# Another plan for the finishes of batches in a Mamba and expert-routing kernel: by when their rows are next written

## The chip, the cores and the metric

The kernel runs on one core of a Trainium2 chip. The time is the device time of one execution in microseconds; the median of several runs is compared. The engines are TensorE (PE; its weight loads are PEld), VectorE (DVE), ScalarE (ACT), GpSimd (POOL) and SyncE (SP, which only issues DMAs here; SPq is its queue). Each works through its own instructions in a fixed order and waits on semaphores for the others.

## What is computed

A layer over 32 batches of 512 tokens of width 256, in fp32. First a Mamba block with an MLP behind it, then eight experts with two chosen for each token, and a shared expert:

```python
x = _layernorm(x + mamba_and_mlp(x))         # conv, selective scan over 512 tokens x 16 states, gate, MLP
scores = softmax(xf @ gate_w.T); _, idx = top_k(scores, 2)
y      = silu(x @ wg[e]) * (x @ wu[e]) @ wd[e]     # for the two experts e of each token
routed = sum over the two of weight * y
shared = silu(xf @ sg.T) * (xf @ su.T) @ sd.T
x = _layernorm(x + routed + shared)
```

The scan is `h = exp(dt * A) * h + (dt * x) * B` over the tokens, for 512 channels and 16 states, then `y = sum over the states of h * C`.

## The kernel before

The 32 batches go through one after another. **The scan** of a batch has 16 states (n) times 4 blocks of 128 channels (j), 64 scan instructions on DVE (L1248, `hs`). For each, ACT makes dA (L779, `ps<-dt,A`) and POOL makes dBx for two at a time (L613, `dBx<-dtx,Bbc`, 32 a batch, three buffers). SP loads the rows of B, spread over the partitions, into four buffers Bbc (L463). TensorE turns `hs` (L991), and DVE adds it into `acc` with C (L1264). Ahead of its scans, each batch needs `dt` and `dtx` in two halves, on POOL (L597, L601), behind ACT's softplus. The steps before and behind the scan of other batches (`pre`, `post`) are interleaved with it.

**The experts.** Batches are put together in groups of 6, 6, 6, 6, 4, 2, 1, 1 (`groups`, `first` is a group's first batch). `post` scatters each token's row to two rows of `X_slots`, sorted by expert (L648, indirect DMAs on POOL). When a group is complete, DVE computes where each expert's tiles begin (the bookkeeping, `meta`), and its tiles of 128 rows go through the experts in pairs (`pairs_in`). SP loads weights `wx` and rows `xin` (L508, L514) and writes the results to `Y_slots` (L531). Groups take turns in two such arrays, so the results of a group overwrite the rows of an earlier one (`before`). Ahead of that SP waits until the rows of the earlier group's last batch have been gathered (L528).

**The finish** of a batch f is what this case is about. SP waits until the store of finish f - 1 has landed (L547), and loads what the shared expert left into the one buffer `fx` (L548). POOL adds the two results of each token to it with eight accumulating gathers from `Y_slots` (L672). ACT takes sums (L914) and squares (L708), POOL computes the scale (L577 to L586, four small operations), ACT applies it (L921) and stores to `out`. That is one SP load, twelve POOL instructions, twelve ACT operations and a store.

**The order** on each engine is fixed when the kernel is built. Every strand of work (scan, pre, post, experts, results, finish, ...) has a table of places in ticks, `AT`, and there are 64 ticks to a batch. `weave` emits the steps of all strands of an engine by 64 * b + place, where b is the period that the step is planned for; a strand never goes back, a later step stands at the place of the one before it or later. The planner fills `pairs_in[b]` and `fins_in[b]`. A period has three places for finishes (0, 1, 2), a single one takes place 0, two take 0 and 1. On POOL they are

```python
"POOL_finish": [142.4813, 143.8018, 145.8918, 147.9589, ...     # place 0: eight gathers, two small steps
                ... 182.6585, 184.3464, 186.0575, 188.6853, 189.1587, 195.0384, 195.6057, 197.2903, 204.1521, 205.4386]
"SP_finish": [140.1056, 161.3954, 177.9993]                     # the load of fx, places 0, 1, 2
```

The line that the change touches says how many finishes a period gets (L187): one, from period 23 on two, from period 27 on three, as far as batches are ready.

Of the kernel before, what the change touches and what calls it, by code (L numbers as in the profile page):

```python
# [9 lines left out]
def group_sizes(n):  # L10

    sizes = []
    for size in (1, 1, 2, 4):
        if n > size:
            sizes.append(size)
            n -= size
    while n:
        sizes.append(min(6, n))
        n -= sizes[-1]
    return sizes[::-1]  # L20
# [112 lines left out]
def build(nc, a, out):  # L133
# [5 lines left out]
    NB, T, D = a["x"].shape  # L139
# [19 lines left out]
    groups = group_sizes(NB)  # L159
    NG = len(groups)  # L160
    first = [sum(groups[:g]) for g in range(NG)]
# [11 lines left out]
    before = [g - 4 if g >= NG - 2 else g - 2 for g in range(NG)]  # L173
# [4 lines left out]
    PERIODS, PAIRS_MAX, FINS_MAX, NR = NB + 3, 12, 3, 3  # L178
    pairs_in, fins_in = [[None] * PAIRS_MAX for _ in range(PERIODS)], [[None] * FINS_MAX for _ in range(PERIODS)]
    ended, finished = 0, 0  # L180
    for b in range(first[0] + groups[0] - 1, PERIODS):
        g = min(sum(first[g] + groups[g] - 1 <= b for g in range(NG)), NG - 1)
        waiting = pairs_to[g - 1] - ended
        left = max(groups[g] - (b - first[g] + 1), 1)
        take = min(waiting, PAIRS_MAX, -(-waiting // left))
        ready = sum(groups[g] for g in range(NG - 1) if pairs_to[g] <= ended) + (groups[NG - 1] if b >= NB else 0)
        done = min(ready - finished, 1 if b < NB - 9 else 2 if b < NB - 5 else 3)  # L187

        for i in range(take):
            pairs_in[b][i * PAIRS_MAX // take] = ended + i  # L190
        for i in range(done):
            fins_in[b][i * FINS_MAX // done] = finished + i
        ended, finished = ended + take, finished + done
# [1336 lines left out]
```

## Time and profile before

| | before |
|---|---|
| median of 3 runs | 4866.85 us (4865.31 to 4877.16) |
| profiled execution | 4879.34 us, span 4877.6 us |
| DVE busy | 4230.3 us (87%) |
| TensorE busy | 4114.6 us (84%) |
| ACT busy | 3579.0 us (73%) |
| POOL busy | 3566.2 us (73%) |

The span is what the profiled execution's instructions cover; its own time is 1.7 us longer. In the rows of stretches (`A:B length`, us from the span's start) stand, for each engine, the busy time and in brackets the number of instructions, then TensorE's granted clock as a share of 2.4 GHz, the mean busy share of the DMA engines, and GB/s. In rows of the timeline stand the start, the time that the row covers, engine, line, operation, what is written and read, and how many instructions the row stands for; in square brackets the idle time of the engine ahead of it and what ended it. In rows of waits stand who waited for whom, the sum in us, how many times, and the longest.

### The profile page before, as it was taken

The numbers are of one execution on the slowest core, as the hardware profiler recorded it, in microseconds if no ns is written. First come the engines' busy times: TensorE is split into PE (matmuls) and PEld (weight loads), VectorE is DVE, ScalarE is ACT, GpSimd is POOL, SyncE is SP. The second block draws the span as 40 slices with busy tenths as digits, with TensorE's granted clock in tenths as the row PEclk, the third lists the DMA queues.
The fourth block names the chain that finished last, engine by engine and source line by source line (L and its number), as shares of the span: only waits on it lengthen the run. The fifth ranks groups of instructions, "written<-read, shape, count | busy, mean of one in ns | idle before, by whom it ended". The sixth has DMA issues, their size and how long they took to land. (4 is left out here: it accounts for less than half of the span.)

```text
span 4877.6 us, 76499 instructions
## 1 busy us (share of the span) xinstructions
PE 4114.6 (84%) x21374; PEld 2848.8 (58%) x21374; DVE 4230.3 (87%) x6070; ACT 3579.0 (73%) x6521; POOL 3566.2 (73%) x2235
## 2 busy tenths in 40 slices
PE   3788888888888888888888888888888889888878
PEld 2455555555656665656665555665556666666565
DVE  4899999888988988998899999888999888898782
ACT  4767777777767777777788777787777787677754
POOL 4667677666666677777788777878778887688865
PEclk7999999999999999999999999999999999999999
DMA  2122422434334234333333333333334553455665
GB/s 92 48 88 86 116 87 78 115 118 139 117 117 132 94 119 119 91 101 118 94 98 106 99 107 105 102 100 111 100 106 127 137 138 116 121 156 157 181 164 117
DMA packets 348901, 550.96 MB, mean 113 GB/s; under 512 B 39345, under 2 KB 197170, under 8 KB 348354
## 3 DMA queue, kind: packets, MB, share of 16 engines
q1 hardware_dynamic: 279650, 448.40, 30.3%
q0 software_dynamic: 47616, 65.17, 6.6%
q10 hardware_dynamic: 21216, 32.51, 1.8%
q8 instruction: 177, 2.90, 0.2%
q14 instruction: 242, 1.98, 0.1%
HBM read 432.26 MB, written 180.80 MB: 126 GB/s over the span
## 5 line engine op out<-in xcount | busy, mean ns | idle before, releaser
L613 POOL TENSOR_TENSOR dBx<-dtx,Bbc 128x1024 f32<-128x1024 f32 x1024 | 2462.0, 2449 | 548.6 <-DVE hs L1248 528.7
L1248 DVE TENSOR_TENSOR_SCAN hs<-ps,dBx 128x512 f32<-128x512 f32 x2048 | 2400.8, 1206 | 233.8 <-ACT ps L779 134.0
L779 ACT ACTIVATE ps<-dt,A 128x512 f32<-128x512 f32 x2048 | 1392.8, 689 | 431.5 <-DVE hs L1248 398.2
L991 PE MATMUL ps<-ident,hs 128*128 128x128 f32 x8192 | 1270.8, 286 | 473.8 <-DVE acc L1264 345.6
L991 PEld LDWEIGHTS ps<-ident,hs 128*128 128x128 f32 x8192 | 954.2, 145 | 955.9 <-DVE acc L1264 589.8
L1264 DVE SCALAR_TENSOR_TENSOR acc<-ps,C_tok,acc 128x512 f32<-128x512 f32 x1664 | 1180.2, 735 | 160.4 <-PE ps L991 148.3
L648 POOL DMA_INDIRECT X_slots<-xs,slots x248 | 247.8, 999 | 268.0 <-DVE slots L1389 203.6
L672 POOL DMA_INDIRECT fx<-Y_slots,slots x224 | 354.0, 1580 | 70.2 <-issue 41.7
L1237 DVE SCALAR_TENSOR_TENSOR xc<-ps,conv_w,xc 128x511 f32<-128x511 f32 (+2 forms) x384 | 285.9, 745 | 48.6 <-ACT xc L743 39.7
L1155 PE MATMUL ps<-xsT,wx 128*128 128x128 f32 x2432 | 316.2, 279 | 5.2 <-ACT xsT L873 4.8
L1155 PEld LDWEIGHTS ps<-xsT,wx 128*128 128x128 f32 x2432 | 295.2, 194 | 34.0 <-issue 32.2
L956 PE MATMUL ps<-xnT,w_in 128*128 128x512 f32 x512 | 262.6, 632 | 45.1 <-DVE xc L1237 44.2
L1008 PE MATMUL ps<-xnT,w_in 128*128 128x512 f32 x512 | 279.7, 649 | 0.0
L1075 PE MATMUL ps<-w_m,post_tmp 128*128 128x256 f32 x1024 | 262.2, 379 | 0.0
L1058 PE MATMUL ps<-mT,w_m 128*128 128x512 f32 x512 | 242.0, 611 | 20.1 <-ACT mT L827 20.1
L597 POOL TENSOR_TENSOR dt<-dt,dtx 128x1024 f32<-128x1024 f32 x64 | 153.4, 2397 | 138.8 <-ACT dtx L770 138.8
L1042 PE MATMUL ps<-w_out,xc 128*128 128x256 f32 x1024 | 253.3, 379 | 0.0
L743 ACT ACTIVATE xc<-ps,conv_b,conv_w 128x512 f32<-128x512 f32 x128 | 99.5, 777 | 192.3 <-PE ps L956 192.3
L1042 PEld LDWEIGHTS ps<-w_out,xc 128*128 128x128 f32 x1024 | 190.3, 190 | 23.6
L1170 PE MATMUL ps<-wx,ge 128*128 128x256 f32 x608 | 166.5, 397 | 43.9 <-DVE ge L1404 42.6
L1075 PEld LDWEIGHTS ps<-w_m,post_tmp 128*128 128x128 f32 x1024 | 184.5, 190 | 20.5
L1028 PE MATMUL ps<-ident,acc 128*128 128x128 f32 x1024 | 179.7, 278 | 0.0
(222 smaller groups left out, 6237.8 us busy)
## 6 DMA issues: line engine op xcount, KB each, us to landing
Bbc<-B_scratch SPq DMA_DIRECT2D x512, 256.0 KB, 3.9
wx<-in_experts SPq DMA_DIRECT2D x304, 384.0 KB, 4.0
Y_slots<-zeros SPq DMA_DIRECT2D x228, 256.0 KB, 4.7
xin<-X_slots SPq DMA_DIRECT2D x304, 128.5 KB, 3.3
Y_slots<-xin SPq DMA_DIRECT2D x304, 128.0 KB, 1.7
xt<-in_x SPq DMA_DIRECT2D x32, 512.0 KB, 4.5
shared<-xt ACTq DMA_DIRECT2D x30, 512.0 KB, 3.9
fx<-shared SPq DMA_DIRECT2D x28, 512.0 KB, 5.3
```

The costliest lines, as they stand in the source:

```text
L613: pool.tensor_tensor(dBx[u % 3][:], dtx[b % 2][:, 2 * h:2 * h + 2, :], Bbc[g % NBB][:, n % CH:n % CH + 1, :].broadcast_to([P, 2, T]), ALU. ...
L672: pool.indirect_dma_start(out=to_finish(f)[:, t, :], out_offset=None, in_=Y_slots[g % 2], in_offset=bass.IndirectOffsetOnAxis(ap=slots[:, ...
L779: act.activation(psA[s % 2][:], dt[b % 2][:, j, :], ACT.Exp, scale=A[:, j, n:n + 1]).then_inc(s_dA, 1)
L956: i = pe.matmul(bank(b, j)[:], w_in[:, k, j * P:(j + 1) * P], xn[:, k, :], start=(k == 0), stop=(k == KD - 1))
L991: i = pe.transpose(psH[w % 2][:, j * P:(j + 1) * P], hs[(n * CT + j) % NHB][:, t * P:(t + 1) * P], ident[:])
L1008: i = pe.matmul(psG[j % 2][:], w_in[:, k, DI + j * P:DI + (j + 1) * P], xn[:, k, :], start=(k == 0), stop=(k == KD - 1))
L1042: i = pe.matmul(psG[q][:, t * D:(t + 1) * D], c[:, k, (2 * q + t) * P:(2 * q + t + 1) * P], w_out[:, k, :], start=False, stop=(k == CT - 1))
L1075: i = pe.matmul(psG[q][:, t * D:(t + 1) * D], post_tmp[:, k, (2 * q + t) * P:(2 * q + t + 1) * P], w_m2[:, k, :], start=False, stop=(k == ...
L1155: i = pe.matmul(psE[:, o * HALF + m * P:o * HALF + (m + 1) * P], w[:, m, (2 * k + o) * P:(2 * k + o + 1) * P], xsT[:, (m * KD + k) * P:(m ...
L1237: dve.scalar_tensor_tensor(out=c[:, j, s:], in0=bank(b, j)[:, 0:T - s], scalar=conv_w[:, j, NK - 1 - s:NK - s], in1=c[:, j, s:], op0=ALU.m ...
L1248: dve.tensor_tensor_scan(hs[s % NHB][:], psA[s % 2][:], dBx[s // 2 % 3][:, s % 2, :], 0.0, ALU.mult, ALU.add).then_inc(s_scan, 1)
L1264: dve.scalar_tensor_tensor(out=o, in0=psH[w % 2][:], scalar=C_tok[b % 2][:, t, n:n + 1], in1=o, op0=ALU.mult, op1=ALU.add).then_inc(s_weig ...
```

## The change

The number of finishes in a period no longer follows from the period's number. For each group h whose results will overwrite rows of an earlier group, and that isn't complete yet, `due` holds how many finishes are still missing until that earlier group is through, and how many periods are left. The period takes the largest quotient, at least one, at most three. The tables of places, the pairs and all else stay.

```diff
         ready = sum(groups[g] for g in range(NG - 1) if pairs_to[g] <= ended) + (groups[NG - 1] if b >= NB else 0)
-        done = min(ready - finished, 1 if b < NB - 9 else 2 if b < NB - 5 else 3)
+        due = [(first[before[h]] + groups[before[h]] - finished, first[h] + groups[h] - 1 - b) for h in range(NG - 1)
+               if before[h] >= 0 and first[h] + groups[h] - 1 > b]
+        due.append((NB - finished, NB - b))
+        done = min(ready - finished, max([1] + [-(-n // max(left, 1)) for n, left in due]), FINS_MAX)
```

Batches finished in each period:

| period | 11 to 13 | 14 to 16 | 17 to 19 | 20 to 22 | 23 | 24 | 25 | 26 | 27 and on |
|---|---|---|---|---|---|---|---|---|---|
| before | 1 each | 1 each | 1 each | 1 each | 2 | 2 | 2 | 0 | 3, 3, 3, 3, 1, 1 |
| after | 2 each | 0 | 2 each | 0 | 3 | 3 | 0 | 0 | 3, 3, 3, 3, 1, 1 |

The lines behind the change move by 3 in the file, so that L597 becomes L600, L613 L616, and L672 L675. Two places on POOL, in its own order. The first is the change from batch 25 to batch 26: dt and dtx are those of batch 26, `dBx` ahead of them belongs to batch 25, and `fx<-Y_slots,slots` are gathers of a finish. Before:

```order
L648 DMA X_slots<-xs,slots 29184x257 x4
L613 TENSOR_TENSOR dBx<-dtx,Bbc 128x1024 x7
L597 TENSOR_TENSOR dt<-dt,dtx 128x1024
L601 TENSOR_TENSOR dtx<-dt,xc 128x1024
L613 TENSOR_TENSOR dBx<-dtx,Bbc 128x1024
L597 TENSOR_TENSOR dt<-dt,dtx 128x1024
```

After:

```order
L616 TENSOR_TENSOR dBx<-dtx,Bbc 128x1024 x3
L675 DMA fx<-Y_slots,slots 128x256
L616 TENSOR_TENSOR dBx<-dtx,Bbc 128x1024 x2
L675 DMA fx<-Y_slots,slots 128x256 x3
L616 TENSOR_TENSOR dBx<-dtx,Bbc 128x1024
L675 DMA fx<-Y_slots,slots 128x256
L616 TENSOR_TENSOR dBx<-dtx,Bbc 128x1024
L600 TENSOR_TENSOR dt<-dt,dtx 128x1024
L604 TENSOR_TENSOR dtx<-dt,xc 128x1024
L675 DMA fx<-Y_slots,slots 128x256 x2
L616 TENSOR_TENSOR dBx<-dtx,Bbc 128x1024
L675 DMA fx<-Y_slots,slots 128x256
```

The eight gathers of the third finish of a period (place 2) now stand there; seven of them come ahead of the first dBx of batch 26. The second place is the middle of batch 13, after the scale of the first finish. Before:

```order
L613 TENSOR_TENSOR dBx<-dtx,Bbc 128x1024 x6
L625 TENSOR_SCALAR ve_post<-mv 128x4
L626 TENSOR_SCALAR nb_post<-mv 128x4
L628 TENSOR_TENSOR rs_post<-ve_post,m_half 128x4
L630 TENSOR_TENSOR nb_post<-nb_post,rs_post 128x4
L613 TENSOR_TENSOR dBx<-dtx,Bbc 128x1024 x4
```

After:

```order
L616 TENSOR_TENSOR dBx<-dtx,Bbc 128x1024 x4
L675 DMA fx<-Y_slots,slots 128x256 x2
L616 TENSOR_TENSOR dBx<-dtx,Bbc 128x1024
L675 DMA fx<-Y_slots,slots 128x256
L616 TENSOR_TENSOR dBx<-dtx,Bbc 128x1024
L628 TENSOR_SCALAR ve_post<-mv 128x4
L629 TENSOR_SCALAR nb_post<-mv 128x4
L631 TENSOR_TENSOR rs_post<-ve_post,m_half 128x4
L633 TENSOR_TENSOR nb_post<-nb_post,rs_post 128x4
L616 TENSOR_TENSOR dBx<-dtx,Bbc 128x1024
L675 DMA fx<-Y_slots,slots 128x256
```

A second finish (place 1) has come in there, away from the change of batch; its last four gathers stand a little further on.

## Rows read from the trace of the kernel before

**Rows 1.** The page: busy time, share of the span and instructions of each engine.

```profile
PE 4114.6 (84%) x21374; PEld 2848.8 (58%) x21374; DVE 4230.3 (87%) x6070; ACT 3579.0 (73%) x6521; POOL 3566.2 (73%) x2235
```

**Rows 2.** Busy time by stretch: batches 7-12, 13-18, 25-27, 28, 29, 30.

```profile
1026.80:1901.70 874.90, 758.48 (x3974) 523.79 (x3972) 782.57 (x1108) 635.20 (x1103) 585.38 (x343) 0.97 0.38 118
1901.70:2769.60 867.90, 750.63 (x3973) 518.70 (x3972) 782.09 (x1108) 667.38 (x1223) 671.68 (x415) 0.98 0.35 103
...
3637.40:4084.80 447.40, 396.77 (x2154) 284.25 (x2154) 399.19 (x560) 361.67 (x700) 379.06 (x244) 0.97 0.48 133
4084.80:4238.50 153.70, 135.33 (x718) 96.22 (x718) 136.51 (x205) 109.40 (x194) 97.84 (x58) 0.94 0.38 112
4238.50:4398.80 160.30, 141.42 (x794) 103.24 (x794) 137.90 (x194) 126.58 (x250) 133.54 (x87) 0.98 0.59 159
4398.80:4568.60 169.80, 144.72 (x786) 105.72 (x786) 142.42 (x210) 129.56 (x258) 143.21 (x95) 0.94 0.57 154
```

**Rows 3.** Waits of DVE, batches 7 to 12, then batches 13 to 18.

```profile
DVE hs L1248 <- ACT ps L779: 33.7, 28, 2.6
...
DVE hs L1248 <- ACT ps L779: 29.1, 26, 2.7
...
DVE hs L1248 <- POOL dBx L613: 2.5, 4, 0.7
```

**Rows 4.** Busy time by stretch: batch 11, batch 12 (with bookkeeping).

```profile
1611.20:1754.20 143.00, 124.38 (x648) 85.99 (x646) 128.87 (x181) 104.44 (x182) 97.45 (x57) 0.96 0.38 117
1754.20:1901.70 147.50, 125.65 (x648) 85.46 (x646) 134.15 (x200) 104.57 (x182) 98.03 (x58) 0.97 0.34 104
```

**Rows 5.** Waits of SP's queue, 3600 to 4240 us.

```profile
SPq L547 <- DMA out<-fx: 35.3, 3, 12.0
```

**Rows 6.** Timeline of POOL around the change from batch 26 to 27.

```profile
3901.47 7.02 POOL L613 TENSOR_TENSOR dBx<-dtx,Bbc 128x1024 f32<-128x1024 f32 x3
...
3923.76 2.37 POOL L597 TENSOR_TENSOR dt<-dt,dtx 128x1024 f32<-128x1024 f32 x1 [3.31 <-ACT dtx L770]
...
3928.70 2.35 POOL L613 TENSOR_TENSOR dBx<-dtx,Bbc 128x1024 f32<-128x1024 f32 x1
```

**Rows 7.** Timeline of DVE, first scans of batch 27.

```profile
3935.16 2.33 DVE L1248 TENSOR_TENSOR_SCAN hs<-ps,dBx 128x512 f32<-128x512 f32 x2
3939.15 2.34 DVE L1248 TENSOR_TENSOR_SCAN hs<-ps,dBx 128x512 f32<-128x512 f32 x2 [1.66 <-ACT ps L779]
```

**Rows 8.** Timeline of POOL around the change from batch 29 to 30.

```profile
4362.53 6.99 POOL L613 TENSOR_TENSOR dBx<-dtx,Bbc 128x1024 f32<-128x1024 f32 x3
4369.68 1.64 POOL L672 DMA_INDIRECT fx<-Y_slots,slots  x1 [0.16 <-issue]
...
4395.77 2.94 POOL L613 TENSOR_TENSOR dBx<-dtx,Bbc 128x1024 f32<-128x1024 f32 x1
```

**Rows 9.** Timeline of DVE, first scans of batch 30.

```profile
4398.79 2.34 DVE L1248 TENSOR_TENSOR_SCAN hs<-ps,dBx 128x512 f32<-128x512 f32 x2 [2.65 <-POOL dBx L613]
4407.86 2.34 DVE L1248 TENSOR_TENSOR_SCAN hs<-ps,dBx 128x512 f32<-128x512 f32 x2 [6.73 <-issue]
```

**Rows 10.** Busy time, sixteen scans around the start of batches 27, 29, 30, 31.

```profile
3915.54:3950.71 35.17, 30.44 (x199) 23.15 (x198) 29.08 (x36) 32.80 (x52) 28.14 (x14) 1.00 0.40 122
...
4218.89:4257.17 38.28, 32.20 (x212) 24.71 (x211) 29.98 (x37) 34.58 (x58) 27.35 (x13) 1.00 0.54 158
4376.43:4421.99 45.56, 36.56 (x215) 28.02 (x214) 30.21 (x38) 39.04 (x74) 40.41 (x24) 0.89 0.60 156
4545.16:4590.57 45.41, 36.07 (x215) 27.30 (x214) 30.20 (x38) 37.12 (x66) 39.80 (x23) 0.92 0.67 182
```

**Rows 11.** Waits of SP's queue in the stretch of batch 30.

```profile
SPq L547 <- DMA out<-fx: 32.8, 3, 24.9
...
SPq L528 <- DMA fx<-Y_slots,slots: 0.7, 1, 0.7
```

**Rows 12.** Waits of SP's queue over the whole span.

```profile
SPq L528 <- DMA fx<-Y_slots,slots: 3.6, 2, 2.8
```

## The prediction, made before the result was known

> **What bounds the kernel now.** I read the page first: the share of busy time puts VectorE (DVE) at 87% over the span, TensorE at 84%, GpSimd (POOL) and ScalarE (ACT) at 73% [rows 1]. Then the span by stretches, each from the first scan of one batch to that of a later one. Six stretches with no finish (batches 7 to 12) take 874.9 us with 782.6 us of DVE work; the next six, with one finish in each batch, take 867.9 us with 782.1 us of it [rows 2]. So the length of a batch follows DVE: 130 us of work in 145. One finish puts (671.68 - 585.38) / 6 = 14.4 us on POOL and (667.38 - 635.20) / 6 = 5.4 us on ACT, none on DVE, and the batch is no longer for it. What DVE waits for says the same: in six batches with one finish it waits 2.5 us in all for POOL's dBx, and 29.1 us for ACT's dA, against 33.7 us for dA in the six without a finish [rows 3]. A finish is covered work, as long as POOL delivers dBx in time.
>
> **What moves.** The planner puts finishes planned for period b where batch b + 2 is scanned: POOL has 343 instructions in batches 7 to 12 and 415 in the next six, twelve more for each, and the first finish is planned in period 11 [rows 2]. Working through the loop, with groups of 6, 6, 6, 6, 4, 2, 1, 1 batches, gives in scanned batches: before, one finish in each of 13 to 24, two in each of 25, 26, 27, none in 28; after, two in 13 to 15, none in 16 to 18, two in 19 to 21, none in 22 to 24, three in 25 and 26, none in 27 and 28. From batch 29 on both plans are alike (18 finishes are placed by then). TensorE and DVE keep their instruction order throughout; POOL, ACT and SP change theirs. The amount of work is the same.
>
> **Edit 1: six batches get a second finish (place 1).** Place 1 exists in batches 25 to 27 now, so its price can be read there. Those three take 447.4 us, 149.1 each, with 7 pairs of expert tiles; batch 28, with 7 pairs and no finish, takes 153.7 us, of which the bookkeeping at the end of a group is 147.5 - 143.0 = 4.5 (batch 12 against 11) [rows 2, 4]. So 149.1 with two finishes against 153.7 - 4.5 = 149.2 with none: price 0. POOL has room: 379.1 of 447.4 us busy in the three [rows 2]. SP waits 35.3 us in three pieces there for the store before a reload of fx [rows 5]; what is queued behind it on SP are the loads of Bbc, wx and xin, and since the three batches are no longer than batch 28 without its bookkeeping, the four Bbc buffers cover it. Six of these at 5 pairs: I take 0, bounds -1 to +1.5 us each.
>
> **Edit 2: seven batches lose theirs.** 16 to 18, 22 to 24 and 27. The nearest rows are the stretch without finishes, 7.0 us per six longer than with them [rows 2]. That stretch also clears Y_slots (DMA share 0.38 against 0.35), so I don't read it as a gain of finishes; it only says that taking one away gives nothing visible. I take 0. The bound below is all of DVE's waiting for dA and dBx in such a batch, (29.1 + 2.5) / 6 = 5.3 us each; the bound above is 7.0 / 6 = 1.2 us each.
>
> **Edit 3: batches 25 and 26 get a third (place 2).** This is the term that isn't zero. POOL_finish starts place 2 at 182.66 ticks and ends it at 205.44, with 64 ticks to a batch, so its eight gathers stand in POOL's queue across the change from one batch to the next, where POOL must also do dt and dtx of the new batch (four operations of 2.4 us) before DVE can scan it. Now this happens twice, into batches 30 and 31. First the change into batch 27, with no place 2: from the last triple of dBx (3901.47) POOL still waits, 3.31 us just before dt, since ACT is later than it; its first dBx for the new batch ends at 3931.06, some 4.1 us before DVE takes it at 3935.16 [rows 6, 7]. Into batch 30 the same chain (from 4362.53) holds seven gathers, the first at 4369.68 (1.64 us), and dBx beside them takes 2.94 instead of 2.35 us; the first dBx for the new batch ends at 4398.71, 36.2 us after the start of the triple instead of 29.6, DVE takes it at once (2.65 us of wait), and the second half comes late: DVE is idle 6.73 us before the scan at 4407.86 [rows 8, 9]. From the first pair of scans to the second it is 9.07 us instead of 3.99 [rows 7, 9].
>
> Those stretches differ in pairs (10 against 7), so I take the price from whole stretches, eight scans either side of the change of batch [rows 10]. Into 27 (7 pairs, no place 2) it lasts 35.2 us; into 29 (10 pairs to come, no place 2) 38.3; into 30 and 31 (place 2) 45.6 and 45.4, with DVE's work the same as into 29 (30.2 against 30.0). **7.2 us for a place 2 with pairs held equal**, 10.3 with them not (45.5 - 35.2). Two of them: 14.4 us, bounds 0 and 20.6. After the change of batch a part can be won back where DVE would have waited for something else. Idle time of DVE outside that stretch: batch 29 has 160.3 - 137.9 - 8.3 = 14.1, batch 30 has 169.8 - 142.4 - 15.4 = 12.0 [rows 2, 10]. So up to 2 us a time come back: 14.4 - 4 = 10.4. On the other side stands what place 2 does to batch 26 beyond that: the reload of fx at its head must wait until ACT has stored the finish before it. In batch 30 SP waits 24.9 us for that and 32.8 in three pieces [rows 11], with Bbc, wx and xin behind it. DVE loses little there (that is inside batch 30's own 12.0), and with 7 pairs there is less behind it; I add 0 to 2 us, once, and take 1. The middle of 10.4 and 14.4 is 12.4, and with that 1 it is 13.4: **+13 us** for this edit.
>
> In the stretches into 30 and 31 TensorE's granted clock is 0.89 and 0.92, into the others 1.00, so in part of them it ran at 1.2 GHz and not 2.4, and its busy time is 36.6 us for 215 matmuls against 32.2 for 212 [rows 10]. This lies inside the 7.2 us. The Trainium skill, page "TensorE: Matmul & The Clock Gate", section "Part 1: The HAM clock gate", says that the clock falls to half after the array has been idle; by that rule the fall follows from the stall, and comes back with it at the two new places. By a clock that fell there for another reason (the 10 pairs), up to 36.6 - 32.2 = 4.4 us of each 7.2 would not recur, and the sum would be 13 - 8.8 = +4.
>
> **Edit 4: the wait that the plan is about.** Before a group's results overwrite Y_slots, SP waits for the gathers of an earlier group (L528). Such waits are 3.6 us in two pieces over the whole span; one of them, 0.7 us, is in the stretch of batch 30, where the plan doesn't change [rows 11, 12]. For groups 2, 3 and 4 the places say that the last finish is on time: SP_results starts at 99.19 ticks of period 17, which is tick 1187, and the gathers of batch 5, planned in period 16, end by tick 1174. Gain: 0.
>
> **Sum.** 0 + 0 + 13 + 0 = +13 us on the profiled execution, whose span is 4877.6 and whose own time is 4879.34. It lies 12.5 us above the median of the runs, 4866.85. On the median: 4880.
>
> **Rivals.** *Place 2 costs nothing at 7 pairs.* The stalls into 30 and 31 would belong to the pairs, the clock or the last groups. For it: batches 25 and 26 have less for SP and TensorE, and part of the extra time is TensorE's at the lower clock. Against it: the stretch into 29, and POOL's chain, which has the same order and no pair in it. Time: -3 to +6, or 4864 to 4873; it decides whether POOL reaches dt in time. *Starved by SP.* With 7 pairs DVE uses up Bbc faster than in batch 30 (149 us a batch against 165), and 25 us of SP's wait outlast the buffers; a third finish also delays the second one, and batch 26 stretches as 30 and 31 did as a whole, with 27.4 us of DVE idle instead of 15: two times 12. Time: +21 to +35, 4888 to 4902. POOL waited only briefly for Bbc in batch 30, so it is unlikely. *Faster.* Seven batches without a finish lose more than half of DVE's waiting for dA and dBx, since ACT is 5.4 us and POOL 14.4 us freer there: 7 x 3 = 21 us, less a small place 2, -10 to -25 and 4842 to 4857. It decides itself from 2 us a batch up. Against it: the 33.7 us of waits for dA in the six batches without finishes. *The plan doesn't move what it says.* The order of POOL shows that it does; no chance.
>
> **How the numbers follow.** The forecast (+6 to +20) has 0.62, nothing 0.20, starved 0.10, faster 0.08. A measurement of this kernel can tell about 0.3% from no change, 14.6 us, so the forecast lies just under that line: of its 0.62 I put 0.27 above it. Slower: 0.27 + 0.10 = 0.37; faster 0.07, a hundredth of that case falling inside; same 0.56. The range holds the forecast and nothing: 4861 to 4889.
>
> **What would show it.** Right: no waits of POOL before dt into batches 26 and 27, DVE idle some 6 us before the third scan there, both stretches of sixteen scans at 42 to 46 us instead of 35.2, TensorE's clock under 1.00 in them, batches 16 to 18 within 2 us of now, and all from batch 28 on unchanged. Wrong: those stretches at 35 to 37 us (nothing), POOL waiting for Bbc by several us in batch 26 (starved), or batches 16 to 18 and 22 to 24 at 142 us or less (faster).

## The result: slower by 0.77%, and where the time is

The changed kernel takes 4918.6 us (median of 5 runs, 4906.69 to 4924.05), the kernel before, beside it, 4873.3 us: 1.0077 times as long, 95% interval 1.0061 to 1.0094. The forecast was 4880, with a range up to 4889. The span of the profiled execution went from 4877.6 to 4917.7 us. The first line of the page of the changed kernel, which answers to [rows 1]:

```profile
PE 4134.5 (84%) x21374; PEld 2873.8 (58%) x21374; DVE 4246.6 (86%) x6070; ACT 3582.7 (73%) x6521; POOL 3567.9 (73%) x2235
```

DVE is busy for 16.3 us more with the same 6070 instructions in the same order. Nothing in the prediction accounts for that. The stretches of the changed kernel show where it is: batches 13 to 15 (two finishes each), 16 to 18 (none), 19 to 21 (two), 22 to 24 (none), and 25 to 27 (three, three, none):

```profile
1905.40:2353.90 448.50, 380.82 (x2012) 266.45 (x2010) 400.51 (x547) 353.17 (x676) 379.21 (x243) 0.97 0.42 115
2353.90:2784.90 431.00, 371.29 (x1964) 257.10 (x1962) 392.31 (x561) 315.65 (x548) 293.75 (x171) 0.98 0.28 87
2784.90:3231.50 446.60, 381.61 (x2012) 266.06 (x2010) 399.56 (x548) 353.29 (x676) 378.96 (x244) 0.97 0.42 116
3231.50:3661.10 429.60, 372.23 (x1987) 258.98 (x1986) 392.80 (x563) 316.56 (x550) 294.94 (x172) 0.99 0.29 88
3661.10:4123.30 462.20, 404.09 (x2154) 291.35 (x2154) 395.99 (x560) 361.84 (x700) 378.98 (x244) 0.96 0.46 129
```

The same stretches of the kernel before. Those of batches 25 to 27 are in [rows 2]:

```profile
1901.70:2338.30 436.60, 379.63 (x2011) 262.57 (x2010) 389.81 (x548) 335.53 (x616) 335.76 (x208) 0.98 0.36 104
2338.30:2769.60 431.30, 371.01 (x1963) 256.13 (x1962) 392.29 (x562) 331.84 (x608) 335.93 (x208) 0.98 0.35 102
2769.60:3202.30 432.70, 377.09 (x2011) 262.77 (x2010) 389.28 (x547) 335.61 (x616) 335.72 (x207) 0.98 0.36 105
3202.30:3637.40 435.10, 376.07 (x1988) 259.25 (x1986) 393.98 (x563) 332.23 (x610) 337.72 (x208) 0.98 0.36 101
```

The two runs of three batches with a second finish lose 11.9 and 13.9 us, and DVE's busy time there grows by 10.7 and 10.3. Batches 16 to 18 stay as they were (431.0 against 431.3), 22 to 24 are 5.5 us shorter. Batches 25 to 27 lose 14.8 us. The kernel before isn't at its best in these rows: TensorE's clock fell for 6.8 us in its batches 14, 15 and 21, at 2.6 to 2.9 us each (the experiments come back to this), so the second finishes cost more than 11.9 and 13.9 us. The rest, 3.7 us ahead of batch 13 and 1.6 from batch 28 on, lies where the two kernels have the same order on every engine; it is within what two executions of one kernel differ by (the spans of e4_before_psum and e9_psum_again below, one kernel, are 9.2 us apart).

Within a batch the loss of place 1 is at one point. Counting from the first scan of batch 14, the two kernels are within 0.4 us of each other up to the 41st scan; from there to the 45th it takes 27.58 us instead of the 21.7 us of batches 16, 17, 22 and 23, which have none, and of the kernel before with one finish. (The last batch of a group, 18 or 24, has the bookkeeping there and takes 26.7 to 26.8 us in both.) In the six batches with a second finish these four scans take 26.3 to 27.6 us, 30.6 us more than six times 21.65. The timeline of DVE there, changed kernel:

```profile
2147.87 0.20 DVE L1350 TENSOR_REDUCE ps<-ps 128x4 f32<-128x32 f32 x1
2148.11 0.19 DVE L1352 TENSOR_TENSOR r<-rank,ps 128x32 f32<-128x32 f32 x1
2148.33 3.10 DVE L1366 TENSOR_TENSOR chosen<-r,r 128x32 bf16<-128x32 f32 x1
2151.45 0.75 DVE L1369 TENSOR_TENSOR prefix<-prefix,chosen 128x8 bf16<-128x8 bf16 x4
...
2160.21 0.42 DVE L1289 SCALAR_TENSOR_TENSOR post_tmp<-post_tmp,ps 128x256 f32<-128x256 f32 x1 [1.32 <-ACT post_tmp L854]
```

The same step in batch 14 of the kernel before:

```profile
2139.96 0.19 DVE L1363 TENSOR_TENSOR chosen<-r,r 128x32 bf16<-128x32 f32 x1
```

And POOL over those microseconds, first the changed kernel, then the kernel before:

```profile
2146.10 5.26 POOL L616 TENSOR_TENSOR dBx<-dtx,Bbc 128x1024 f32<-128x1024 f32 x2
...
2154.53 1.08 POOL L651 DMA_INDIRECT X_slots<-xs,slots  x1 [2.94 <-DVE slots L1392]
...
2159.08 0.19 POOL L585 TENSOR_SCALAR ve_fin<-squares_fin 128x4 f32<-128x4 f32 x1 [2.19 <-ACT squared L711]
```

```profile
2133.63 2.36 POOL L613 TENSOR_TENSOR dBx<-dtx,Bbc 128x1024 f32<-128x1024 f32 x1 [0.52 <-DVE hs L1248]
2143.27 1.12 POOL L648 DMA_INDIRECT X_slots<-xs,slots  x1 [7.29 <-DVE slots L1389]
```

`chosen` adds two small tiles, `one1` and `one2`, both in SBUF. It takes 3.10 us instead of 0.19, and ends 0.06 us after POOL's second dBx (2151.36). Before, POOL had done its dBx 4 us earlier and stood idle for 7.29 us, waiting for `slots`, while DVE did this step. The eight gathers of place 1 take up POOL's idle time (2.94 us of that wait are left): POOL's last two dBx slip until they lie over `chosen`. In all six batches with a second finish (13 to 15, 19 to 21) `chosen` takes 2.98 to 3.84 us, and each time it ends 0.06 us after the second of two dBx of POOL. The wait is inside the instruction, so it is booked as busy and stands in no list of waits. The group of that line, changed kernel:

```profile
L1366 DVE TENSOR_TENSOR chosen<-r,r 128x32 bf16<-128x32 f32 x31 | 34.9, 1125 | 1.1
```

**Place 2** came as forecast. Sixteen scans around the start of batches 26, 27 and 28 of the changed kernel, which answer to [rows 10]:

```profile
3789.41:3832.89 43.48, 34.10 (x200) 25.22 (x198) 29.22 (x36) 37.48 (x70) 41.27 (x25) 0.92 0.46 119
3949.11:3992.14 43.03, 33.83 (x200) 24.91 (x198) 29.46 (x36) 37.14 (x70) 40.37 (x24) 0.92 0.57 154
4103.65:4138.81 35.16, 30.43 (x199) 23.14 (x198) 29.07 (x35) 32.77 (x52) 28.14 (x14) 1.00 0.35 106
```

43.5 and 43.0 us against 35.2, with the same work on DVE, and TensorE's clock at 0.92. Inside the first of them POOL doesn't wait before `dt`, and DVE stands idle ahead of the third scan of batch 26, as the prediction said (some 6 us):

```profile
3813.05 2.34 DVE L1251 TENSOR_TENSOR_SCAN hs<-ps,dBx 128x512 f32<-128x512 f32 x2 [2.72 <-POOL dBx L616]
3822.14 2.34 DVE L1251 TENSOR_TENSOR_SCAN hs<-ps,dBx 128x512 f32<-128x512 f32 x2 [6.75 <-issue]
```

### The profile page after: what moved, and what is told of

Read it like the earlier page. It is cut to its first block and busy times, and to the rows that moved or that the text cites. A ratio compares the mean times of both kernels' runs of the same rounds, so it can differ in the third digit from the quotient of the medians.

```text
span 4917.7 us, 76499 instructions
## 1 busy us (share of the span) xinstructions
PE 4134.5 (84%) x21374; PEld 2873.8 (58%) x21374; DVE 4246.6 (86%) x6070; ACT 3582.7 (73%) x6521; POOL 3567.9 (73%) x2235
## 5 line engine op out<-in xcount | busy, mean ns | idle before, releaser
L616 POOL TENSOR_TENSOR dBx<-dtx,Bbc 128x1024 f32<-128x1024 f32 x1024 | 2464.6, 2444 | 580.9 <-DVE hs L1251 565.1
L675 POOL DMA_INDIRECT fx<-Y_slots,slots x224 | 354.2, 1581 | 75.9 <-issue 40.5
L600 POOL TENSOR_TENSOR dt<-dt,dtx 128x1024 f32<-128x1024 f32 x64 | 155.7, 2433 | 132.1 <-ACT dtx L773 132.1
L1045 PEld LDWEIGHTS ps<-w_out,xc 128*128 128x128 f32 x1024 | 190.3, 190 | 23.6
```

What stands on the lines that cost most here:

```text
L616: pool.tensor_tensor(dBx[u % 3][:], dtx[b % 2][:, 2 * h:2 * h + 2, :], Bbc[g % NBB][:, n % CH:n % CH + 1, :].broadcast_to([P, 2, T]), ALU. ...
L675: pool.indirect_dma_start(out=to_finish(f)[:, t, :], out_offset=None, in_=Y_slots[g % 2], in_offset=bass.IndirectOffsetOnAxis(ap=slots[:, ...
L1045: i = pe.matmul(psG[q][:, t * D:(t + 1) * D], c[:, k, (2 * q + t) * P:(2 * q + t + 1) * P], w_out[:, k, :], start=False, stop=(k == CT - 1))
```

## The experiments

**The two parts of the change, one at a time.** e1_doubles keeps the new plan up to period 22, e2_triples from 23 on:

```diff
 # e1_doubles
         done = min(ready - finished, max([1] + [-(-n // max(left, 1)) for n, left in due]), FINS_MAX)
+        if b > 22:
+            done = min(ready - finished, 2 if b < NB - 5 else 3)
 # e2_triples
+        if b < 23:
+            done = min(ready - finished, 1)
```

> The change in periods 11 to 22 only (two finishes in 11 to 13 and in 17 to 19, none in the three periods behind each), from period 23 on the plan of before (2, 2, 2, 0). My theory after the result: a second finish in a batch with 5 pairs costs 4.7 to 5.8 us at the chosen operation and just behind it, so six times about 5.2 us, 31 us, some 4904 us beside 4873 for the kernel before. The theory of the prediction (place 1 is free, place 2 costs 7 us) expects no change, 4870 to 4878. In the profile I expect the sum over chosen (128x32, bf16) on DVE to be in excess by 3.0 to 3.8 us in batches 13, 14, 15, 19, 20, 21, and the stretches of sixteen scans into batches 26 and 27 to be 35.2 us as before.

> The other part of the change alone: one finish a period up to 22, then three in 23 and 24 and none in 25 and 26. My theory: two finishes in place 2 cost 8 us each at the change of batch, so +12 to +17 us, some 4887 us beside 4873. If the two parts don't add up (a starved queue only when both are there), this is +0 to +5 us and the doubles alone too little as well. Profile: sixteen scans around the start of batches 26 and 27 last 43 us, chosen is 0.19 us in batches 13 to 24.

Measured beside the kernel before at 4881.1 us: e1_doubles 4906.6 us, 1.0057 (1.0038 to 1.0077), some 28 us; e2_triples 4895.7 us, 1.0030 (1.0016 to 1.0045), some 15 us. Together 43 us, for 37 (by the ratio) to 45 us (by the medians) of the whole change; the two parts add up. So two thirds of the loss come from the second finishes, which the prediction had at nothing, and one third from the third ones, which it had at 13. In the profile of e1_doubles `chosen` is 3.0 to 3.9 us in batches 13 to 15 and 19 to 21, and the three batches take

```profile
1904.11:2353.29 449.18, 383.09 (x2012) 267.03 (x2010) 400.01 (x547) 353.31 (x676) 379.08 (x243) 0.97 0.43 115
```

The sixteen scans into its batches 26 and 27 are 35.2 and 35.4 us, as expected. In the profile of e2_triples batches 25 to 27 take 460.1 us instead of the 447.4 of [rows 2], and 13 to 15 take 431.1, with `chosen` at 0.19 in all of batches 13 to 24.

**Taking the cause away.** e3_after_psum is the changed kernel, e4_before_psum the kernel before, each with this edit. A copy of `one2` is made in PSUM, `chosen` reads it there, and the sum that `prefix` adds up is made in PSUM as well, so that no operation of this step has two inputs in SBUF. The kernel computes what it did; DVE has two operations more in each batch. (NROUTE is the number of semaphore steps of this part.)

```diff
-        NROUTE, NMETA = 21, 18
+        NROUTE, NMETA = 23, 18
...
+                    if b < NB - 1:
+                        dve.tensor_tensor(rest, rank[:], wide(key2), ALU.is_equal).then_inc(s_route, 1)
+                        dve.wait_ge(s_route, done + 17)
...
-                    dve.tensor_tensor(chosen[:], one1[:], one2[:], ALU.add).then_inc(s_route, 1)
+                    dve.tensor_tensor(chosen[:], one1[:], rest, ALU.add).then_inc(s_route, 1)
+                    dve.tensor_tensor(eq, one1[:], rest, ALU.add).then_inc(s_route, 1)
                     for t in range(NTB):
-                        dve.wait_ge(s_route, done + 17 + t)
-                        dve.tensor_tensor(prefix[:, t + 1, :], prefix[:, t, :], chosen[:, t, :], ALU.add).then_inc(
+                        dve.wait_ge(s_route, done + 19 + t)
+                        dve.tensor_tensor(prefix[:, t + 1, :], prefix[:, t, :], eq[:, t, :], ALU.add).then_inc(
```

> The changed kernel, with the operations chosen and prefix on DVE reading one of their two inputs from PSUM and not both from SBUF. For that two operations of 128x32 (about 0.2 us each) are added in each batch, so about 0.45 us x 31 = 14 us of DVE work more. Theory A (chosen waits there because GpSimd's dBx holds the port that a second SBUF input needs): chosen is 0.2 us in every batch, the 28.9 us of excess are gone, so about 28.9 - 14 = 15 us faster than the changed kernel, and if the whole loss of place 1 hangs on it, up to 22 us. Theory B (chosen waits for something else, a semaphore or GpSimd's result, and is only where it shows): it is 3 us long as before and the kernel is 14 us slower than the changed one.

> The kernel before with the same exchange of inputs, the reference for the run above. Theory A: its 14.8 us of excess (batches 25, 26, 29, 30, 31) are gone and 14 us of work are added, so 4873 within 6 us. The difference between the changed plan and the plan before, with the exchange in both, is then 45 - 14 = 31 us if the rest of the loss in place 1 stays, and 15 to 20 us if all of it hangs on chosen. Theory B: 14 us slower than before, and the difference stays at 45 us.

e3_after_psum takes 4883.9 us, 1.0002 (0.9990 to 1.0014) of the kernel before: the changed plan with the exchange is as fast as the plan before without it. e4_before_psum takes 4860.3 us, 0.9960 (0.9947 to 0.9974), below the 4873 within 6 us that was expected: the exchange helps the plan before as well, whose batches 25, 26 and 29 to 31 have a long `chosen` too. With the exchange in both, the changed plan still costs 23.6 us, between the 15 to 20 expected if all of place 1 hangs on `chosen` and the 31 if only the instruction does; in the two profiles 18 of these lie in batches 25 to 27. So of the loss, place 2 stays and much of place 1 is gone. Theory A holds and theory B falls. The line of `chosen` in e3_after_psum, all 31 of them (shortest, median, longest in ns, then first and last start):

```profile
L1369 DVE TENSOR_TENSOR chosen<-r,ps x31: 186/186/190, 284.2 to 4679.8; 128x32 bf16<-128x32 f32 x31
```

That isn't because `chosen` has moved to where POOL is idle: in nine batches, 13 to 15 and 19 to 21 among them, it lies wholly inside one of POOL's dBx and takes 186 to 189 ns.

The four scans from the 41st to the 45th of batch 14 (two finishes) and batch 16 (none), first in the changed kernel, then in e3_after_psum:

```profile
2138.30:2165.88 27.58, 20.79 (x92) 14.51 (x90) 23.53 (x52) 15.48 (x36) 20.33 (x17) 0.87 0.43 108
2438.03:2459.68 21.65, 17.32 (x87) 11.81 (x86) 20.32 (x51) 10.84 (x17) 12.31 (x9) 1.00 0.32 110
```

```profile
2139.69:2161.73 22.04, 17.36 (x87) 11.72 (x86) 20.97 (x53) 15.49 (x36) 18.96 (x16) 1.00 0.56 135
2426.95:2448.93 21.98, 17.36 (x87) 11.73 (x86) 20.62 (x53) 10.84 (x17) 12.32 (x9) 1.00 0.36 109
```

With the inputs exchanged the second finish costs 0.06 us there (at most 0.6, in batch 21), though ACT does as much for it as before and POOL nearly so. So the whole step of 4.7 to 5.9 us hangs on `chosen`: 2.8 to 3.7 us in the instruction, and the rest goes with it. That the rest comes of `slots` being later, of POOL's scatters behind it and of TensorE's clock, 0.87 to 0.94 in these four scans of the six batches, is my reading and wasn't tested by itself. The added work costs 0.3 us a batch (21.98 against 21.65). The gain was larger than the 15 to 22 us expected, 35 us against the changed kernel. Nine long `chosen` (13 to 15, 19 to 21, 29 to 31) are gone, 28.9 us of excess, and with the six of place 1 what followed them.

**Any operation with two inputs in SBUF?** e6_prefix_sbuf is e3_after_psum with the additions of `prefix` reading `chosen` (SBUF) again instead of `eq` (PSUM).

> As e3_after_psum, but only chosen reads PSUM; the first of the four prefix additions behind it reads both inputs from SBUF again. Theory A (any DVE operation with two inputs from SBUF waits for the GpSimd operation that is running): chosen is 0.2 us everywhere, and the wait of 2 to 4 us turns up at prefix in batches 13 to 15, 19 to 21, 29 to 31. The time is that of the changed kernel plus the added operations, some 5 to 12 us, so 4923 to 4930, and 35 to 45 us above e3_after_psum. Theory B (it is something about chosen alone, its bf16 output or its place): prefix stays at 0.16 us each and the time is that of e3_after_psum, 4884.

4928.2 us beside 4879.5, 1.0107 (1.0085 to 1.0130), as expected: the loss is back, some 0.3% above that of the changed kernel (1.0077), which has two operations fewer in a batch. Its two lines:

```profile
L1369 DVE TENSOR_TENSOR chosen<-r,ps x31: 186/186/188, 284.6 to 4717.2; 128x32 bf16<-128x32 f32 x31
L1373 DVE TENSOR_TENSOR prefix<-prefix,chosen x124: 161/163/5392, 284.9 to 4723.4; 128x8 bf16<-128x8 bf16 x124
```

`chosen` never waits, `prefix`, which was 0.16 us throughout in the changed kernel, takes 2.4 to 3.0 us once in each of batches 13 to 15, 19 to 21, 29 and 30, 1.2 in 25, and 5.4 in 31. The wait goes to the first operation with both inputs in SBUF, whichever it is.

**Place 2.** e5_moved is e2_triples with the third finish of period 24 moved to places 24 ticks later, on POOL (from its first gather) and on ACT. (The change in `weave` that takes a table for each period is left out here.)

```diff
+def moved(table, late):
+    return lambda b: late if b == 24 else table
...
-                  (finish(), AT["POOL_finish"]))
+                  (finish(), moved(AT["POOL_finish"], AT["POOL_finish"][:20] + [v + TICKS for v in AT["POOL_finish"][:10]])))
...
-                  (finish(), AT["ACT_finish"]), (last(), AT["ACT_last"]))
+                  (finish(), moved(AT["ACT_finish"], AT["ACT_finish"][:24] + [v + TICKS for v in AT["ACT_finish"][:12]])), (last(), AT["ACT_last"]))
```

> As e2_triples (one finish a period up to 22, three in 23 and 24), but the gathers and the steps behind them of the third finish of period 24 stand 24 ticks later, at places that place 0 has in period 25, in which there is no finish. Nothing is left out. Theory: place 2 costs because its gathers keep GpSimd from dt, dtx and the first dBx of the next batch. Then sixteen scans around the start of batch 27 last 35 to 37 us as with no place 2, and those around batch 26, where place 2 stays, 42 to 43 us; the whole is 6 to 8 us faster than e2_triples, 4888 against 4895.7. Rival: the cost belongs to the third finish itself (more gathers, more for ACT, in a batch that is full), then the stretch around 27 loses nothing or the loss turns up within batch 27, and the time stays 4893 to 4899.

Sixteen scans around the start of batch 26, where place 2 stays, and 27, where it is gone:

```profile
3755.28:3797.36 42.08, 33.60 (x200) 25.06 (x198) 29.15 (x35) 37.54 (x70) 40.03 (x24) 0.92 0.46 118
3914.74:3950.17 35.43, 30.45 (x199) 23.15 (x198) 29.16 (x36) 33.02 (x53) 28.17 (x14) 1.00 0.45 138
```

The stall and the lower clock are gone from the second and not from the first. So the price of place 2 at the change of batch is that of its position. POOL's and ACT's steps were moved together; that it is POOL's order rests on its timeline (the gathers stand ahead of the new batch's first dBx), and no run moved one without the other. The whole kernel, 4885.9 us and 1.0023 (1.0009 to 1.0037), is less clear: the expected 6 to 8 us to e2_triples (1.0030) are within the two intervals, and so is no gain at all. In the profiles batches 25 to 27 take 459.4 us instead of 460.1, 7.5 us of stall less being mostly made up for by two of the falls of the clock told of below, 2.7 us each, in batches 26 and 27, and by a longer batch 25 (152.1 us against 150.6).

**Is the second finish free then?** e7_doubles_psum is e1_doubles with the exchange of inputs. Its time was that of the second case expected and its scans those of the first, so it was run once more beside e4_before_psum, as e8_doubles_again and e9_psum_again.

> The plan of e1_doubles with the exchange of inputs of e3 and e4. If the whole price of a second finish in a batch with 5 pairs hangs on chosen, the time is that of e4_before_psum (the plan before, same exchange), 4860 within 6 us, and the four scans from the 41st to the 45th of batches 13 to 15 last 22.0 us as in batch 16. If something of it is ACT's or SP's load of the second finish, it is 8 to 15 us more, 4868 to 4875, and those scans last 23 to 25 us.

> The kernel of e7_doubles_psum once more, now on one chip with e9. In its profile batches 15 and 21 were 4 us longer than 14 and 20, with TensorE's clock at half for 6.8 us about 116 us into the batch, and its time was 4873 and not the 4860 expected. Theory: where that fall of the clock lands is chance; then another profile shows it in other batches of 13 to 24, up to five of them, about 2.7 us each, and the difference to e9 on the same chip is under 8 us. Rival: the second finish brings it in the third batch of each run of three, then 15 and 21 show it again, and the difference stays 10 to 15 us.

> The kernel of e4_before_psum once more, the plan before with the exchanged inputs. It should be 15 to 22 us faster than the kernel before again, and its profile should show none of the falls of the clock in the same batches as the first time if they are chance (there 17 and 26).

e7_doubles_psum took 4873.4 us, 0.9986 (0.9972 to 1.0000), and not the 4860 of e4_before_psum. On one chip e8_doubles_again took 4868.0 us, 0.9976 (0.9964 to 0.9989), and e9_psum_again 4856.9 us, 0.9951 (0.9935 to 0.9967). So 11 to 13 us remain for the second finishes, a quarter of a per cent, less than half of the 28 us with `chosen` as it was: the exchange took 15 to 17 us of the price of the second finishes away. These sizes are rough, since the intervals of e8 and e9 just overlap. In both pairs of profiles (e7 and e4, e8 and e9) batches 13 to 15 and 19 to 21 are together 10 us longer. In the profile of e7_doubles_psum the 41st to 45th scans are 22.0 to 22.6 us, but batches 15 and 21 have a step further on. The 49th to 57th scans of batches 14 and 15 there:

```profile
2165.23:2178.76 13.53, 11.58 (x46) 5.50 (x46) 13.53 (x16) 11.22 (x20) 13.11 (x7) 1.00 0.73 245
2309.64:2326.10 16.46, 14.87 (x46) 6.65 (x46) 13.85 (x17) 10.92 (x19) 12.85 (x7) 0.79 0.68 199
```

The same 46 matmuls, with the granted clock at 1.00 or 0.79: it fell to the lower level of 1.2 GHz for 6.8 us, and the eight scans take 2.9 us longer. I had expected chance, with under 8 us between e8 and e9; the rival was that it comes in the third batch of each run of three, with 10 to 15 us. The difference, 11 us, is the rival's, the batches are neither's: e8_doubles_again has it in 14 and 21, e7 in 15 and 21, while e4 and e9 have it in none of those six batches; but e3_after_psum, which has the same second finishes, has it in none either, and the kernel before has it in 14, 15 and 21 with one finish each. The three batches 13 to 15 take 436.5 us in e8 and 431.0 in e9, 430.7 in e3. Whether that is chance or comes of the plan, and what makes the clock fall there, stays open, and with it the cause of the 11 to 13 us.

## Why the prediction was wrong

- **What bounds the kernel now**: right that it is DVE, and wrong in how that was used. A finish puts no instruction on DVE, and I took that for putting no time on it. Its gathers delay POOL's dBx, and a dBx that runs beside `chosen` holds DVE up.
- **Edit 1, the second finish: the step that failed.** Forecast 0, bounds -1 to +1.5 us each, 9 us for six; measured 28 us, 4.7 us each (e1_doubles). This alone carries the result out of the range. What the runs showed in place of the 0 is a wait inside DVE's `chosen` for POOL's dBx, 2.8 to 3.7 us a batch and 4.7 to 5.9 with what goes with it; the exchange took 15 to 17 of the 28 us away, and the cause of the 11 to 13 left is open. I priced it by the length of batches 25 to 27 against batch 28 less its bookkeeping, and batch 28 wasn't a clean reference. Its 41st to 45th scans, in the kernel before, take 30.18 us with the clock at 0.81, where in the other batches with bookkeeping (12, 18, 24) they take 26.8:

```profile
4168.50:4198.68 30.18, 24.23 (x109) 17.42 (x110) 26.17 (x71) 12.44 (x21) 14.74 (x12) 0.81 0.16 48
```

  In the changed kernel batch 28, with the same orders and no such fall there, takes 150.2 us; less 4.5 that is 145.7, and 149.1 for two finishes would have read as a price of 3.4 us and not as 0.

  And batches 25 to 27 themselves already paid: their `chosen` takes 0.83, 3.28 and 0.19 us. Both were to be had before. In the groups of the trace of the kernel before stood

```profile
L1363 DVE TENSOR_TENSOR chosen<-r,r 128x32 bf16<-128x32 f32 x31 | 20.8, 669 | 1.1
```

  669 ns on average for an operation on 32 elements a partition, beside 162 for `prefix`: 14.8 us above 31 times its median of 0.19, all in five batches with a second finish (25, 26, 29, 30, 31). The page of the Trainium skill "SBUF — State Buffer", section "SBUF: two separate sides", states the rule: a DVE operation with two SBUF inputs and a GpSimd operation that reads SBUF exclude each other for a whole instruction. The trace agrees that `chosen` doesn't run beside a dBx: it ends 0.06 us after one. It differs in how long that lasts. By the page whichever starts first goes first, while here `chosen` also waits for a second dBx, which starts after it: 3.84 us in batch 15, where one dBx takes 2.94 to 2.96. An estimate from batch 26 of the kernel before, whose `chosen` is 3.1 us too long, would have been six times 3.1 us more, +31 us in all with the 13. I had looked at the scans alone, which read one input from PSUM.
- I also took the list of what DVE waits for as proof that nothing held it up. It can't show this kind of wait.
- **Edit 2, seven batches without a finish**: forecast 0, right for 16 to 18 (431.0 against 431.3). The 5.5 us gained in 22 to 24 are falls of the clock that the profiled execution of the kernel before happened to have there (batches 22 and 24).
- **Edit 3, place 2**: forecast 13.4 us, measured 15 (e2_triples, 8 to 22). Sixteen scans came at 43.5 and 43.0 us where 42 to 46 were expected, and e5_moved shows that the position makes them so. That part of the chain was also right in the clock there (0.92), which fell with the stall and was back at 1.00 where the stall was gone. But I let the fall of the clock follow from the stall, and the stall also comes without it. Of the 22 stretches into batches 30 and 31 in the eleven profiles, 17 take 43.9 to 46.0 us with the clock at 0.89 to 0.96, and 5 take 41.4 to 41.5 us with it at 1.00, with place 2 in all. So up to 4 of the 7.2 us that I priced from them belong to the lower clock and not to the stall alone.
- **Edit 4, the wait that the plan frees**: 0, as forecast; nothing in any run speaks of a gain. In the changed kernel these waits are 4.3 us in two pieces, against 3.6 in [rows 12].
- **The rivals**: none was the one that came true. The one that ended slowest, "starved", reached to 4902 and rested on waits for Bbc; POOL didn't wait for Bbc in batch 26 of the changed kernel.

## What to carry to other kernels

Work moved into the idle time of one engine isn't free for another that shares something with it: look at what the other engine executes at that moment, not only whether anyone waits. In the groups of a profile, compare an instruction's mean with that of its neighbours of the same size; a mean of several times the median can be a wait booked as work (here 669 ns against 191), and an input moved to PSUM took it away. Queued work placed across the start of a loop's next round delays that round's first operations: it cost 8 us here, and moving it away took that stall out, though the gain for the whole kernel wasn't clear of noise.

## What the runs showed of the hardware

- A DVE operation on 128x32 elements with both inputs in SBUF takes 0.19 us beside an idle POOL, and 2.4 to 5.4 us when POOL multiplies 128x1024 tiles in SBUF back to back. It ends 0.06 to 0.09 us after POOL's operation, and isn't let in between two that follow each other closely (31 of 31 such cases in the five profiles without the exchange). With one input in PSUM it takes 0.186 to 0.190 us, also in the 51 cases, in six profiles, where it lies wholly inside such an operation of POOL.
- Eight scans take 13.5 us at full clock and 16.1 to 16.5 us when TensorE's clock falls to 1.2 GHz for 6.8 us in them, in the same kernel from batch to batch. The four falls of 3.4 us that lie wholly in these eight scans cost 1.3 us each (14.81). One of 3.4 us some 34 us into a batch costs next to nothing: batches 19 to 22 of e4_before_psum, with such a fall, take 143.4 us, and 14 and 15, without, 143.2. One profiled execution has up to six of the long ones in batches 13 to 24 (e2_triples; five before, one in the changed kernel).
- The exchange of inputs alone, with the plan of before, is worth 0.4 to 0.5% (0.9960 and 0.9951 of the kernel before, on two chips), although it adds two operations a batch. That is faster than both kernels that were compared here.
